# QKV of a decoder layer with the weights stationary and the tokens moving, rotation out of PSUM on VectorE, low parts on GpSimd, and two of eight FFN weight blocks decoded in a later stage

## What is computed

```python
qkv = x @ w_qkv                                  # 1024 -> 32 query heads, 8 key and 8 value heads of 32
xq, xk = _apply_rope(xq), _apply_rope(xk)        # pairs (x1, x2) of a head: x1*cos - x2*sin, x1*sin + x2*cos
probs = jax.nn.softmax(jnp.where(causal, xq @ xk.T * scale, -jnp.inf), axis=-1)
x = _layernorm(x + (probs @ xv) @ w_o)
x = _layernorm(x + cross_attention(x, ctx))      # Q = x Wq + bq, K = ctx Wk + bk, attended = softmax(QK^T/32) ctx
w_l = dequant_kbit(qweight, lut4, 4)             # 1024 x 1024 weights from 4 bit planes and 16-entry tables
x = _layernorm(x + (x @ w_l.T + bias))           # the row norms stay under the threshold for the 8-bit weights
```

## Time and profile before

| | |
|---|---|
| time, median of 3 runs | 1388.21 us (1386.46 to 1388.99) |
| the profiled execution: its own time, its span | 1388.76 us, 1387.0 us |
| PE busy | 1321.6 us (95%) |
| DVE busy | 924.8 us (67%) |
| ACT, POOL busy | 549.7 us (40%), 543.5 us (39%) |
| mean granted clock of TensorE | 0.971 of 2.4 GHz |

### The profile page before, as it was taken

One profiled execution on the slowest core, in us unless ns is written; L12 is line 12 of the kernel. 1 busy time (PEld: TensorE's weight loads), 2 busy tenths in 40 slices (PEclk: granted clock), 3 DMA queues, 4 the chain that ended last, 5 costly groups with the idle time before them and its releaser, 6 DMA issues.

```text
span 1387.0 us, 25843 instructions
## 1 busy us (share of the span) xinstructions
PE 1321.6 (95%) x8086; PEld 1070.3 (77%) x8086; DVE 924.8 (67%) x2558; ACT 549.7 (40%) x1633; POOL 543.5 (39%) x467
## 2 busy tenths in 40 slices
PE   7799999999679999999999999999999999999998
PEld 6687777787557777777777778788888888788886
DVE  6988888988787888887888422225353534666665
ACT  4222222222677777877777211224242423200000
POOL 1534343434545565556556100043544442222221
PEclk9899999999769999999999999999999999999999
DMA  7334334334793444434343421202424154522222
GB/s 252 91 116 142 120 116 127 96 119 134 223 260 92 128 117 128 129 116 141 117 125 106 159 84 46 76 1 77 167 77 167 62 182 183 203 88 86 83 86 76
DMA packets 161916, 169.84 MB, mean 122 GB/s; under 512 B 35520, under 2 KB 136128, under 8 KB 161856
## 3 DMA queue, kind: packets, MB, share of 16 engines
q1 hardware_dynamic: 161856, 169.07, 38.4%
HBM read 112.40 MB, written 56.62 MB: 122 GB/s over the span
## 4 chain that ended last, share of the span: by engine, by line
PE 67%; issue 13%; DVE 12%; POOL 3%; ACT 1%; SPq 1%; DMA 1%; DVEq 0%; POOLq 0%; ACTq 0%
PE bank L727 13%; PE bank L569 12%; PE bank L571 12%; PE bank L570 12%; PE bank L673 7%; DVE pick L1327 5%; PE bank L660 4%; POOL x2b L1790 3%; PE bank L700 2%; DVE pick L1316 2%; PE bank L704 2%; DVE rot_s L1278 2%; PE bank L578 1%; PE bank L837 1%; DVE qT_lo L1241 1%
## 5 line engine op out<-in xcount | busy, mean ns | idle before, releaser
L1718 POOL TENSOR_TENSOR prob<-prob,rinv 128x512 f32<-128x512 f32 x192 | 206.7, 1077 | 174.8 <-DVE rinv L1386 174.5
L1038 ACT ACTIVATE prob<-bank,nmax 128x256 f32<-128x256 f32 (+1 forms) x512 | 211.3, 427 | 98.1 <-DVE nmax L1378 88.5
L1378 DVE CUSTOM_DVE_ANT_0 bank<-bank,mask 128x256 f32<-128x256 f32 (+1 forms) x512 | 168.8, 380 | 6.2 <-PE bank L660 3.5
L569 PE MATMUL bank<-w_hi,xT_hi 128*128 128x512 f32 x384 | 157.4, 410 | 4.1 <-DVE w_lo L1241 4.1
L571 PE MATMUL bank<-w_hi,xT_lo 128*128 128x512 f32 x384 | 152.7, 398 | 0.0
L570 PE MATMUL bank<-w_lo,xT_hi 128*128 128x512 f32 x384 | 152.2, 396 | 0.0
L1684 POOL TENSOR_TENSOR rot_c<-raw,tab 128x256 f32<-128x256 f32 (+1 forms) x64 | 83.7, 1317 | 166.1 <-ACT raw L969 126.4
L673 PE MATMUL bank<-ident,prob 128*128 128x128 f32 x768 | 129.3, 294 | 8.8 <-POOL prob L1718 8.4
L673 PEld LDWEIGHTS bank<-ident,prob 128*128 128x128 f32 x768 | 89.8, 147 | 44.4 <-issue 18.6
L660 PE MATMUL bank<-k,q 96*128 96x256 f32 (+1 forms) x512 | 108.6, 317 | 7.0 <-DMA vv<-v_scr 5.6
L969 ACT ACTIVATE raw<-bank 128x512 f32<-128x512 f32 (+1 forms) x48 | 25.3, 527 | 221.9 <-PE bank L571 221.7
(11 more groups left out here) (158 smaller groups left out, 3053.3 us busy)
## 6 DMA issues: line engine op xcount, KB each, us to landing
q<-qk_scr SPq DMA_DIRECT2D x192, 128.0 KB, 2.4
x_st<-x_scr SPq DMA_DIRECT2D x32, 512.0 KB, 4.0
qk_scr<-qT_hi SPq DMA_DIRECT2D x16, 640.0 KB, 3.8
qk_scr<-qT_lo SPq DMA_DIRECT2D x16, 640.0 KB, 3.9
x_st<-x SPq DMA_DIRECT2D x16, 512.0 KB, 3.4
f_scr<-pick SPq DMA_DIRECT2D x16, 512.0 KB, 5.1
y<-x SPq DMA_DIRECT2D x16, 512.0 KB, 3.5
x_scr<-y SPq DMA_DIRECT2D x16, 512.0 KB, 2.8
```

The lines of the kernel that those rows point to most:

```text
L569: nc.tensor.matmul(o, l_hi, r_hi, start=first, stop=False)
L1038: mm = nc.scalar.activation(prob[:, k % 4, i * keys:(i + 1) * keys], SBANK[pos][:, i * keys:(i + 1) * keys], ACT.Exp, bias=nmax[:, k % 4, ...
L1378: mm = nc.vector.tensor_tensor_reduce(part, part, mask[:, 2 * P - keys:2 * P], 1.0, BIGGEST, ALU.add, ALU.min, nmax[:, k % 4, i:i + 1])
L1718: nc.gpsimd.tensor_tensor(pr, pr, rinv[:, k % 4, 0:n].unsqueeze(2).to_broadcast([P, n, keys]), ALU.mult)\
```

## The change

**QKV.** The host passes `x` already transposed (`x_cols`) and `w_qkv` with its columns in another order: five chunks of 256 columns (`PAIRS` = 5), in each the even members of the rotation pairs of 8 heads in the first 128 and the odd ones in the second, and one chunk with the values. The stage runs over four groups of 512 tokens; a group has five pair steps (`qk_pair`: 2 halves x 8 x 3 = 48 matmuls of 128x512, the weights stationary) and one value step (`values`: 8 x 4 x 3 = 96 matmuls of 128x256, the tokens stationary). The result of a pair step stands transposed in two banks of PSUM, so `turn_q` and the token transposes are gone, and `raw`, `turned` with them.

**Rotation.** `rope_pair` is six DVE operations of 128x512 per pair step; four read PSUM alone with the table, and two of these write back to the same bank. ACT writes the high parts (`rope_high`), and POOL subtracts in place for the low parts (`rope_low`), released by the first DVE operation of the next pair (`a_turned`). SP stores four times 256 KB (`store_pair`).

**Tokens.** `x_in` and `x_lo` are one piece of memory, so `load_x` of the next group waits, piece by piece, until `values` has used the old one (`x_used`), and ACT and DVE then split it (`x_high`, `x_low`).

**Decoding.** Six of the eight blocks (`EARLY`) are decoded in the QKV stage in four parts each, one per step (`PARTS_OF`; two in step (1, 2), none in (3, 5)). `turn_f` stands one step behind the step that ends a block (`F_TURN`): steps (0, 4), (1, 2), (1, 5), (2, 3), (3, 1) and (3, 5), written (group, chunk). Blocks 6 and 7 are decoded in the fold (`LATE_PARTS`), with `turn_f` behind `fold` of m = 4 and m = 6 (`F_FOLD`), in memory that `m_hi` takes from m = 6 on, which is why ACT waits there for `pick_step`. The loops of the QKV stage and of the fold are written out.

```diff
+        PARTS_OF = {(g, c): ((1, 1, 1, 1, 1, 1), (1, 1, 2, 1, 1, 1), (1, 1, 1, 1, 1, 1), (1, 1, 1, 1, 1, 0))[g][c] for g, c in ORDER}
+        PART_END = dict(zip(ORDER, itertools.accumulate(PARTS_OF[at] for at in ORDER)))
...
+        F_TURN = {ORDER[i + 1]: b for b, i in DECODED_AT.items()}
...
+        LATE_PARTS = {1: 1, 2: 2, 3: 2, 4: 2, 5: 1}
+        F_FOLD, LATE_FBANK = {4: BATCH - 2, 6: BATCH - 1}, (bank[7], bank[4])
...
+            def load_x(g, kt):
+                if g:
+                    sp.wait_ge(x_used, KT * (g - 1) + kt + 1)
+                sp.dma_start(x_in[:, kt, :], x_cols[g * KT + kt, :, :]).then_inc(xw_ld[kt], 16)
...
+            def store_pair(g, c):
+
+                n = PAIRS * g + c
+                slot, base = n % 2, KCOLS + CHUNK * c if c < PAIRS - 1 else 0
+                sp.wait_ge(r_lo_ready, n + 1)
+                for i, half, t in ((0, 0, 1), (0, 1, 3), (1, 0, 0), (1, 1, 2)):
+                    rows = qk_scr[i, base:base + CHUNK, g * GROUP:(g + 1) * GROUP].rearrange("(p t) s -> p t s", t=2)
+                    sp.dma_start(rows[:, half, :], rot[:, slot, t, :]).then_inc(r_stored[slot], 16)
...
+            for m in range(2, KT):
+                load_wk(m)
+                if m == 4:
+                    sp.wait_ge(codes_ready, 2 * (BATCH - 1))
+                    load_planes(BATCH - 1)
+                if m == 5:
+                    sp.wait_ge(pick_step, PICKS * (BATCH - 1))
+                    load_lut(BATCH - 1)
+                if m == 6:
+                    store_f(BATCH - 2)
+            sp.wait_ge(pick_step, PICKS * BATCH)
...
+            def qk_pair(g, c):
+
+                n = PAIRS * g + c
+                wait(pe, r_ready, n - 1)
+                for kt in range(KT):
+                    if g == 0 and c == 0:
+                        pe.wait_ge(w_lo_ready, kt + 1)
+                    if g == 0 and c == 1 and kt % 4 == 0:
+                        pe.wait_ge(w_lo_ready, KT + kt // 4 + 1)
+                    if g == 0 and c > 1 and kt % 4 == 0:
+                        pe.wait_ge(w_lo2_ready, 2 * (c - 2) + kt // 4 + 1)
+                    if c == 0:
+                        pe.wait_ge(x_lo_ready, KT * g + kt + 1)
+                    for half in range(2):
+                        cols = slice(half * P, (half + 1) * P)
+                        mm = product(PAIR_BANK[n % 2][half][:, :], w_hi[:, c, kt, cols], w_lo[:, c, kt, cols],
+                                     x_hi[:, kt, :], x_lo[:, kt, :], kt == 0, kt == KT - 1)
+                        if kt == KT - 1:
...
+            def values(g):
+
+                wait(pe, v_copied, 2 * g)
+                for kt in range(KT):
+                    if g == 0 and kt % 4 == 0:
+                        pe.wait_ge(w_lo2_ready, 2 * (PAIRS - 2) + kt // 4 + 1)
+                    for t in range(GT):
+                        o = VBANK[t // 2][:, t % 2 * KCOLS:(t % 2 + 1) * KCOLS]
+                        toks = slice(t * P, (t + 1) * P)
+                        for ps in range(3):
+                            mm = nc.tensor.matmul(o, (x_lo if ps == 2 else x_hi)[:, kt, toks],
+                                                  (w_lo if ps == 1 else w_hi)[:, PAIRS, kt, :],
+                                                  start=kt == 0 and ps == 0 and t % 2 == 0,
+                                                  stop=kt == KT - 1 and ps == 2 and t % 2 == 1, skip_group_check=True)
...
+            for at in ORDER:
+                if at[1] < PAIRS:
+                    qk_pair(*at)
+                else:
+                    values(at[0])
...
+                if at in F_TURN:
+                    turn_f(F_TURN[at])
...
-            with pe.Fori(1, KT // 2) as m2:
-                for slot in range(2):
-                    u_row(2 * m2 + slot, slot)
-                    fold(2 * m2 + slot, slot)
+            for m in range(2, KT):
+                u_row(m, m % 2)
+                fold(m, m % 2)
+                if m in F_FOLD:
+                    turn_f(F_FOLD[m], LATE_FBANK)
+            pe.wait_ge(f_lo_ready, 2 * BATCH)
...
+            def x_high(g, kt):
+                act.wait_ge(xw_ld[kt], 16 * (g + 2))
+                copy(x_hi[:, kt, :], x_in[:, kt, :]).then_inc(x_hi_ready, 1)
...
+            def rope_high(g, c):
+
+                n = PAIRS * g + c
+                slot = n % 2
+                act.wait_ge(r_ready, n + 1)
+                copy(rot[:, slot, 1, :].bitcast(F32R), rot[:, slot, 0, :])
+                copy(rot[:, slot, 3, :].bitcast(F32R), rot[:, slot, 2, :]).then_inc(r_hi_ready, 1)
...
+            def values_out(g):
+
+                act.wait_ge(x_used, KT * (g + 1))
                 for j in range(2):
-                    n = 2 * b + j
...
-
-            x_high(0, 0)
+                    wait(act, v_stored, 16 * (2 * g + j))
...
+            for g, c in ORDER:
+                if c < PAIRS:
+                    rope_high(g, c)
+                else:
+                    if g < GROUPS - 1:
+                        for kt in range(KT):
+                            x_high(g + 1, kt)
+                    values_out(g)
+                if g == 0 and c < 3:
+                    w_high(c + 3)
+                if (g, c) in F_TURN:
+                    f_high(F_TURN[g, c])
...
+            for m in range(KT):
+                if m == KT - 2:
+                    act.wait_ge(pick_step, PICKS * BATCH)
+                m_high(m, m % 2)
+                if m < KT - 2:
+                    wk_high(m + 2, m % 2, m // 2 + 2)
+                if m in F_FOLD:
+                    f_high(F_FOLD[m], LATE_FBANK)
...
+            def x_low(g, kt):
+                dve.wait_ge(x_hi_ready, KT * g + kt + 1)
+                low(x_lo[:, kt, :], x_in[:, kt, :], x_hi[:, kt, :]).then_inc(x_lo_ready, 1)
+
+            def rope_pair(g, c):
+
+                n = PAIRS * g + c
+                slot, ty = n % 2, 0 if c == PAIRS - 1 else 2
+                dve.wait_ge(a_done, n + 1)
+                wait(dve, r_stored[slot], 64 * (n // 2))
+                even, odd = PAIR_BANK[slot]
+
+                def times(o, i, t):
+                    pair = lambda w: w.rearrange("p (e s) -> p e s", s=SEQ)
+                    return nc.vector.tensor_tensor(pair(o), pair(i[:, :]),
+                                                   tab[:, ty + t, :].unsqueeze(1).to_broadcast([P, 2, SEQ]), ALU.mult)
+
+                times(rot[:, slot, 0, :], even, 0).then_inc(a_turned, 1)
+                times(even[:, :], even, 1)
+                dve.wait_ge(b_done, n + 1)
+                times(rot[:, slot, 2, :], odd, 0)
+                times(odd[:, :], odd, 1).then_inc(b_turned, 1)
+                dve.wait_ge(b_turned, n + 1)
+                nc.vector.tensor_tensor(rot[:, slot, 0, :], rot[:, slot, 0, :], odd[:, :], ALU.subtract)
+                nc.vector.tensor_tensor(rot[:, slot, 2, :], rot[:, slot, 2, :], even[:, :], ALU.add).then_inc(r_ready, 1)
...
+            for g, c in ORDER:
+                if c < PAIRS:
+                    rope_pair(g, c)
+                if (g, c) in F_TURN:
+                    f_low(F_TURN[g, c])
+                if c == PAIRS and g < GROUPS - 1:
+                    for kt in range(KT):
+                        x_low(g + 1, kt)
+                for part in PARTS[PART_END[g, c] - PARTS_OF[g, c]:PART_END[g, c]]:
+                    for go in part:
+                        go()
...
+            def decode_late(m):
+                first = sum(LATE_PARTS.get(i, 0) for i in range(m))
+                for part in late_parts[first:first + LATE_PARTS.get(m, 0)]:
+                    for go in part:
+                        go()
+            decode_late(1)
+            for m in range(2, KT):
+                u_row(m)
+                m_low(m, m % 2)
+                if m < KT - 2:
+                    wk_low(m + 2, m % 2)
+                if m in F_FOLD:
+                    f_low(F_FOLD[m], LATE_FBANK)
+                decode_late(m)
...
+            def rope_low(g, c):
+
+                n = PAIRS * g + c
+                tile = lambda t: rot[:, n % 2, t, :]
+                pool.wait_ge(r_hi_ready, n + 1)
+                if n + 1 < PAIRS * GROUPS:
+                    pool.wait_ge(a_turned, n + 2)
+                nc.gpsimd.tensor_tensor(tile(0), tile(0), tile(1), ALU.subtract)
+                nc.gpsimd.tensor_tensor(tile(2), tile(2), tile(3), ALU.subtract).then_inc(r_lo_ready, 1)
```

More of the change, by code:

```diff
@@ L22 @@
+import itertools
 import math
@@ L134, in decoder_layer @@
-        sb("pad_slots", [P, 2 * (REP * SEQ + SEQ + 2 * HD) - 2 * ROPE])
-        xT_hi, xT_lo = sb("xT_hi", [P, 2, KT, P], F32R), sb("xT_lo", [P, 2, KT, P], F32R)
-        turned = sb("turned", [P, ROPE])
+        w_hi, w_lo, w_in = parts(a1, "w", [P, PAIRS + 1, KT, CHUNK])
+        x_hi, x_lo, x_in = parts(a1, "xc", [P, KT, GROUP])
+        for i in range(SLOTS - 1):
+            sb(f"pad_slot{i}", [P, REP * SEQ + SEQ + 2 * HD])
+        tab = sb("tab", [P, 4, SEQ])
```

(10 more changed lines are left out.)

453 lines of the change are left out of this document (150 added, 303 removed).

## The result

The changed kernel takes 1351.94 us (median of 4, 1348.43 to 1352.97) beside 1388.2 for the kernel before (median of 4); the ratio is 0.9736, with a 95% interval of 0.9716 to 0.9756. I forecast 1330: the direction and the range hold, and the gain is 36 us instead of 59. The profiled execution has a span of 1351.2.

A forecast was written before the change was run, and what follows sets the result against it. PE was taken as the limit up to the last QKV matmul, with DVE close behind. QKV -55.9, batch 0 -11.2 and fold +8.0 sum to -59.1: 1388.8 becomes 1330 us, range 1314 to 1354, likeliest 1316 to 1346.

The forecast's parts named there:

- PE's work: QKV: matmuls cost 2.1 us more in all, while 36 x 0.84 = 30.2 us of transposes go.
- The start: QKV: PE starts at 6.5 us against 10.56; the lower clock costs 2 and the first pair ends at 19.5.
- DVE's rotation: QKV pair steps: six operations of 0.6 to 0.66 us each, some 3.75 per step with one handover.
- the rival of slow PSUM products: QKV: PSUM products near 0.8 us make DVE the bound, some 2 us per block reach PE: 1342 us, 15%.
- the one that would have made the kernel slower: QKV rotation out of PSUM: from about 1.25 us per operation the gain is gone; about 1395 at 1.30; 4%.
- POOL and SP: QKV: two low-part subtractions of 1.3 us per pair step on POOL, and stores of 4.2 us, hidden by 1 to 3.
- The rival of GpSimd holding DVE up: QKV: POOL's low parts lengthen DVE's decoding by 1.3 us per pair step: 1350 us, 1364 with both operations; 6%.
- The stall at (1, 5): QKV, end of step (1, 5): group 2 starts 10.9 us after `values`, PE stands 10.0, 12.0 in all with lower clock.
- Inside the same cover: QKV: SP's issues of planes, tables and tokens ahead of pair (1, 0)'s store are hidden like the other stores, costing nothing.
- Batch 0: Attention's first batch: three waits gone, -12.6, first row maxima 1.4 later: 66.1 to 54.9 us, -11.2; only some 5 if DMA bounds.
- The `vv` term: Batch 0 of attention: `vv` is stored group by group and no longer late, so PE's wait of 5.6 us goes.
- Fold: Fold: `turn_f` waits 2.1 and 3.1 us for late blocks, plus two `turn_f` and lower clock: +8.0, between 3 and 13.

The follow-up runs named there:

- best3: Changed kernel plus six fixes together (orders on DVE, ACT and fold, `w_low` on DVE, loads spread, values staged apart), and block 6 decoded a step earlier: 1315.55 us.
- experiment 5: Against the changed kernel, `rope_low` on GpSimd runs at once, without its wait for `a_turned`: 1354.88 us, ratio 0.9751.
- experiment 6: Against the changed kernel, SP's 21 attention loads are spread, one unit behind each store of steps (1, 0) to (1, 2): 1351.23 us, ratio 0.9722.
- experiment 7: Against the changed kernel, the second half of the last group's values is staged apart, so ACT skips the first half's store: 1348.58 us, ratio 0.9708.
- Experiments 9 and 10: Against a 1318.19 us kernel with six fixes: attention unit 6's loads issued earlier in batch 0, 1318.74 us; 2 MB more moved there, 1323.74 us.
- experiment 4: Against the changed kernel, DVE copies the next row of b ahead of the decoding parts in the fold: 1344.01 us, ratio 0.9707.

## Why the prediction was right, and by how much it was off

The direction and the range were right, and so was what most terms were made of. Three stages each missed by 4 to 10 us, all to the slow side; the range was wide enough for their sum.

*PE's work* was right to about a microsecond: 0.23 us a matmul, 0.12 a narrow one, 36 x 0.84 of turns gone. The start was better than forecast, 5.80 instead of 6.5, with the first pair done near 18 instead of 19.5: the slower pace, 0.43 us from start to start, lasted 3 us. (I called it the lower clock; the granted clock of those 3 us reads 1.00, so only the pace is shown. Behind the later waits it reads 0.50.)

*DVE's rotation.* I took 0.6 to 0.66 between bounds of 0.3 and 1.3; it is 0.60 (46.07, 46.67, 47.27 above). With it fall the rival of slow PSUM products, and the one that would have made the kernel slower. One figure beside it does not follow from its terms: 11.9 us for a step with the split of a block, where 3.75 + 5.9 + 1.2 are 10.9. The sum does not use it. That DVE was busy for 244 us of the forecast 240 to 260 is luck: without the 15 us of hold-up it is 229, below the range, and best3, with 9.8 us more of its own work and no such hold-up, shows 238.6.

*GpSimd.* The term that failed is the one that is not there. "POOL and SP" counts two subtractions per pair step and leaves out `w_low`, 21 us in group 0, an operation of the changed kernel that stands in its code. (The rival of a bound DVE has "w's low parts about 15" on DVE, where 5.8 us of them stand.) PE waited 7.2 us and lost 0.8 + 1.4 more at the lower clock, 9.4 in all; moving `w_low` to DVE gave 8.3 back. The 10.0 us by which the stage missed are these 9.4 and 3.6 of the stall below, less 1.8 by which the first five pairs ended early (61.8 instead of 63.6) and some 1.2 of smaller terms. The rival of GpSimd holding DVE up, at 6%, had the mechanism, but through `rope_low`; that its 1350 is so near is luck, since it puts all of its 20 us into the QKV stage, and half of the real miss lies elsewhere. Its chance was too low because I weighed it by `rope_low` alone, which the wait for `a_turned` lays beside PSUM work (experiment 5 shows what happens on DVE without it). The row that spoke for it was 2748 against 805. The rule of the Trainium skill named with that rival (page "SBUF — State Buffer", section "🔬 SBUF: two separate sides"), that one of the two engines is shut out for the other's whole instruction, agrees with the two leaves that end 0.5 us after GpSimd's subtractions, and with the longer operations on both engines in experiment 5.

*The stall at (1, 5).* Place and queues were right, the size was not: from the end of `values` to the next group 14.5 us instead of 10.9. I let the token splits run during `values` and only the last one behind it. In fact SP's loads stood behind a store that waits for GpSimd, the first split came 2.7 us after the end, the last 8.6. The values' copies with the store between them took 3.3 (159.25 to 162.53) instead of the 4.2 that I had.

*SP.* "Inside the same cover" was wrong, and its list (planes, tables and tokens) lacks the 21 loads of attention that stand there: their issues take 11.5 us and hold a store for 5, DVE for 4.0 and `turn_f` of (1, 5) for most of 3.0 (experiment 6). Without a row I should have bounded it.

*Batch 0.* Up to the first projection 66.2 us became 60.4, 5.8 less instead of 11.2. Of the three waits that I took off only `turned` went. The tail of the block did not: DVE's wait for ACT's copies of it was 3.5 and is 6.5, and PE's waits for the exponentials grew from 1.4 to 7.7 where I had +1.4, since those copies stand behind the store of the values' first half (2.9 us of it in experiment 7). The `vv` term, -5.6, did not come either: 6.5 us of that wait are there. In sum PE waits as long as before, 20.4 and 20.1 us by the rows; what came off is its busy time, 45.6 against 39.9, for nearly the same number of matmuls, at a granted clock of 0.67 against 0.74. Why the clock is higher is not shown. So the sum was built from the wrong parts there. I had named the cover ("the stretch is at 0.86 of DMA") and the 5 us that would then come off, which is near the 5.8; with the waits as they are, that nearness shows nothing by itself. Experiments 9 and 10 show that one other order does not help there and that bytes cost.

*Fold.* +17.7 instead of +8.0. My count of DVE's work is the one of experiment 4, where the waits are 2.16 and 2.16 for forecast 2.1 and 3.1 and the sum +6.5. What I overlooked is that another PE step, `u_row`, waits for a copy of 0.2 us which stands on DVE behind the same parts (third place of the order, the first `b_rows` behind the five operations), and one m earlier than `turn_f`. It is the same lateness, met at an earlier point where less of it is absorbed: waits of 4.64 and 5.57, with a granted clock of 0.50 for some 4 us behind each.

*The signs.* No `turned`, PE's busy time, the rotation near 600 ns from start to start and the largest wait at (1, 5) came as named. `turn_f` in QKV under 2 us (7.2 and 3.0), two waits of 2 to 3 us in the fold (4.6 and 5.6, for another copy) and the projection 55 us behind the last QKV matmul (60.4) did not.

*The sum.* Misses of +10.0 in QKV, +4.0 in attention and +9.7 in the fold, with -0.4 in the rest, give 1353 from 1330, the time of the profiled execution.
